# A graph network block on one core: node loops written out, chunks of four tiles, units of eight, a ring of six

## The reference

```python
seg = edge_type * N_NODES + dst
def _rgcn_layer(x, W, root, bias, src, dst, seg):
    agg = jax.ops.segment_sum(x[src], seg, num_segments=N_REL * N_NODES)
    agg = agg.reshape(N_REL, N_NODES, -1)
    return jnp.einsum('rnd,rde->ne', agg, W) + x @ root + bias
```

## Time and profile before

| | us |
|---|---|
| Median of 3 runs | 10040.12 (10038.99 to 10089.25) |
| Profiled execution, its span | 10274.9 |
| PE busy | 6298.0 (61%) |
| POOL busy | 4692.1 (46%) |
| DVE busy | 2244.8 (22%) |
| ACT busy | 1095.0 (11%) |

### The profile page before, as it was taken

How to read it: one execution, slowest core, us unless ns; L and a number is a source line. 1 busy time by engine, 2 the same in 40 slices (tenths; PEclk the granted TensorE clock), 3 DMA queues, 4 the chain that set the end, 5 groups by cost and what they waited for, 6 DMA issues and landing times.

```text
span 10274.9 us, 106460 instructions
## 1 busy us (share of the span) xinstructions
PE 6298.0 (61%) x23187; PEld 4307.1 (42%) x23188; DVE 2244.8 (22%) x6475; ACT 1095.0 (11%) x2855; POOL 4692.1 (46%) x4958
## 2 busy tenths in 40 slices
PE   5866556555556666666666665664666665556666
PEld 2333333333333334444444444443444444444445
DVE  2311111111111122222222221222222222222222
ACT  1110000000000000000000000010111111111111
POOL 0134555554555544444444444445444444444443
PEclk9977777777777777777777777777777777777777
DMA  4443333333333333333332323323222222222222
GB/s 120 131 123 95 93 93 98 99 94 93 95 93 96 97 89 89 92 91 91 90 91 87 90 87 93 89 86 97 67 73 67 69 68 71 72 70 69 67 68 60
DMA packets 410721, 899.60 MB, mean 88 GB/s; under 512 B 149828, under 2 KB 236588, under 8 KB 391946
## 3 DMA queue, kind: packets, MB, share of 16 engines
q0 software_dynamic: 232128, 634.17, 21.4%
q10 hardware_dynamic: 116050, 257.82, 8.2%
q1 hardware_dynamic: 62518, 7.30, 0.6%
HBM read 704.42 MB, written 192.01 MB: 87 GB/s over the span
## 4 chain that ended last, share of the span: by engine, by line
PE 38%; issue 29%; another core or an unknown queue 27%; DVE 2%; ACT 2%; ACTq 1%; DVEq 1%; DMA 1%; POOL 0%; POOLq 0%; SPq 0%; PEld 0%; PEldq 0%
PE ps_out L1169 17%; PE ps_y L1130 8%; PE ps_y L1344 3%; PE ps_tr L1286 2%; PE ps_b L1355 2%; PE ps_c L1355 2%; DVE onehot L849 1%; PE ps_tr L1108 0%; PE ps_out L1183 0%; ACT L713 0%; DVEq L849 0%; PE ps_b L1274 0%; PE ps_c L1230 0%; DVEq L885 0%
## 5 line engine op out<-in xcount | busy, mean ns | idle before, releaser
L447 POOL DMA_INDIRECT ring<-table,idx_now x4836 | 4634.1, 958 | 4979.6 <-PEq L1180 3530.7
L1169 PE MATMUL ps_out<-ring,onehot 128*125 x10848 | 3342.2, 461 | 2881.1 <-issue 1772.5
L1169 PEld LDWEIGHTS ps_out<-ring,onehot 128*125 128x125 f32 x10848 | 2290.8, 225 | 3938.9 <-issue 3574.5
L849 DVE TENSOR_TENSOR onehot<-targets,nodes_now 128x250 f32<-128x250 f32 x2712 | 1131.5, 422 | 5341.1 <-remote 2955.1
L1130 PE MATMUL ps_y<-W,hT 128*125 128x512 f32 (+1 forms) x3000 | 1347.1, 600 | 17.5 <-DVE y_stage L739 16.4
L1130 PEld LDWEIGHTS ps_y<-W,hT 128*125 128x125 f32 x3000 | 598.9, 207 | 606.7 <-issue 560.5
L1344 PEld LDWEIGHTS ps_y<-hT,big 128*128 128x128 f32 x3200 | 440.2, 207 | 25.4 <-issue 4.7
L1355 PE MATMUL ps_b<-big,gT 128*125 128x256 f32 x800 | 268.1, 467 | 294.6 <-ACT gT L713 282.2
L1344 PE MATMUL ps_y<-hT,big 128*128 128x125 f32 x3200 | 444.5, 291 | 5.5 <-issue 5.4
L462 ACT COPY y_stage<-ps_y 125x512 f32<-125x512 f32 x450 | 263.5, 585 | 1002.0 <-PE ps_y L1130 973.3
L1286 PE MATMUL ps_tr<-W,gT 128*125 128x256 f32 x800 | 258.2, 493 | 94.6 <-ACT gT L663 94.6
(11 more groups left out here) (172 smaller groups left out, 2819.1 us busy)
## 6 DMA issues: line engine op xcount, KB each, us to landing
table<-y_stage ACTq DMA_DIRECT2D x150, 1008.0 KB
ring<-table,idx_now POOLq DMA_INDIRECT x4836
base_in<-table ACTq DMA_DIRECT2D x150, 125.0 KB
table<-y_stage ACTq DMA_DIRECT2D x150, 117.0 KB
x_in<-in_x_dram ACTq DMA_DIRECT2D x100, 125.0 KB
xn_in<-xn_scratch ACTq DMA_DIRECT2D x100, 125.0 KB
xn_scratch<-xn_in ACTq DMA_DIRECT2D x50, 125.0 KB
res_scratch<-res_win ACTq DMA_DIRECT2D x50, 125.0 KB
```

Source lines behind the costliest of these rows:

```text
L447: nc.gpsimd.indirect_dma_start(ring[:, c * D:(c + 1) * D], None, table[l], bass.IndirectOffsetOnAxis(ap=idx_now[:, c:c + 1], axis=0)).then ...
L849: nc.vector.tensor_tensor(onehot[u][:, :, :], targets[:, bass.ds(col + u * TILES, TILES)].unsqueeze(2).broadcast_to([128, TILES, WIN]), no ...
L1169: mm = nc.tensor.matmul(ps_out[0:WIN, 0:D], onehot[u][:, j, :], ring[:, bass.ds(slot + j * D, D)], start=(start and u == 0 and j == 0), st ...
```

## The change

The five numbers are set anew: four tiles in a chunk (a chunk is 512 edges), two chunks in a unit (eight tiles, 1,024 edges; `UNIT` itself stays), a ring of six chunks (24 tiles, where it was 26), and three chunks in SP's first group of indices. `windows` becomes a Python loop, so that each engine's program holds the 50 windows one after the other; the inner loop over units, whose bounds come from the data, stays a loop.

```diff
-TILES = 2
-RING = 13
+TILES = 4
+RING = 6
 UNIT = 2
-GROUP_A = 7
+GROUP_A = 3
...
-            body((0, 0, 0), None)
-            with eng.Fori(0, NW // 2 - 1) as i:
-                body((i * 2 + 1, 1, i), (i * 2, 0, i))
-                body((i * 2 + 2, 0, i + 1), (i * 2 + 1, 1, i))
-            last = (NW - 1, 1, NW // 2 - 1)
-            body(last, (NW - 2, 0, NW // 2 - 1))
+            last = None
+            for w in range(NW):
+                cur = (w, w % 2, w // 2)
+                body(cur, last)
+                last = cur
             tail(last)
```

## The result

The changed kernel takes **10,888.65 us** (median of 4 runs, 10,888.12 to 10,900.18) against 10,052.5 us (4 runs) for the kernel before: 1.083 times as long, with an interval of 1.081 to 1.085, or 836 us more. I had forecast 355 us more.

A forecast was written before the change was run, and what follows sets the result against it. The prediction put the time in waits between engines, repeated in 147 window steps. Steps +340, padding +75 and register rows -60 gave +355 us, added to the median of 10,040 for 10,395 us; range 9,450 to 11,000.

The forecast's parts named there:

- its matrices wait for late releases: Fifth unit of a layer 1 window: its one-hot matrices wait for PE's signals, 12.5 and 13.6 us late.
- G: Moment in a window's step when the first slots come back and gathers start, 5.8 us after the first matmul.
- 24 gathers, to G + 29.7: POOL in a window: gathers for the fourth to sixth units run without a pause, ending 29.7 us after G.
- the result's signal comes 8.7 us later: From sum's end to ACT: 8.7 us where gathers have started again, the middle of 2.5 and 14.9.
- first rival: Window step: faster by fewer late releases, fifth unit's first chunk waiting only for data; step 55 us, 9,450 us; chance 0.24.
- second rival: Window step: much slower, lateness per matmul or POOL never pausing while signals wait; step 65.5 us, 11,000 us; chance 0.14.
- +2.3 us carried to all layers: Window steps: layer 1's growth from 59.1 to 61.4 us applied to all 147 steps, +340 us.
- The median: Whole kernel: the profiled execution is 2.3% above the median of 10,040 us; the 355 us were added to the median.
- Padding, +75 us: End of each layer: edge list padded to 1,632 gathers instead of 1,612, so the last window ends later, +75 us.
- Register rows, -60 us: Written-out windows: about five register rows a window leave PE's path at 0.08 us each, -60 us.
- Look-ahead: Window start: 16 instead of 22 tiles lie ahead; without late releases this alone would cost 7.5 us more on that path.
- What would show it: New profile's signs: 61.4 us steps in layer 1, runs of 24 gathers, one 10 us pause, 1,632 gathers a layer.

The follow-up runs named there:

- r3: Kernel before with units of eight tiles and a ring of 24, chunks still of two tiles, on chip A: 10,236.3 us, ratio 1.019.
- e8: Changed kernel, but a window's last unit of slots given back only after its transposes (layer 3: next window's start), chip A: 9,724.5 us, ratio 0.967.
- r2: Changed kernel with a window's last slots given back only after the transposes, run again on chip A: 9,728.8 us, ratio 0.969.
- t2: Kernel before, loops kept, with the changed numbers and the last unit's slots given back only after the transposes, chip B: 10,027.3 us, ratio 0.980.
- s2: Kernel before with windows written out, old numbers, and the last unit's slots given back only after the transposes, chip B: 10,081.3 us, ratio 0.989.
- s3: Kernel before, loops kept, with the last unit's slots given back only after the transposes, chip B: 10,150.4 us, ratio 0.995.
- e1: Kernel before with only the loops over windows written out, numbers as before, chip A: 10,009.5 us, ratio 0.996.
- e3: Kernel before with only the ring one chunk shorter (12 chunks of two tiles), loops kept, chip A: 10,123.3 us, ratio 1.008.
- e4: Kernel before with units of eight tiles and a ring of 24, chunks still of two tiles, chip C: 7,807.5 us, ratio 1.136.
- r4: Kernel before with chunks of one tile, units of four and a ring of 26 tiles, chip A: 10,644.3 us, ratio 1.061.
- e11: Changed kernel with the last unit's slots given back after the transposes, in layer 3 already after the activation's signal, chip C: 8,069.0 us, ratio 1.174.
- e7: Kernel before with chunks of one tile, units of four and a ring of 26 tiles, chip C: 6,819.8 us, ratio 0.992.
- e9: Kernel before with the last unit's slots given back only after the window's transposes, chip C: 6,876.1 us, ratio 1.000.

## Why the prediction was wrong

The direction held, and the time lies in the whole range, but outside the forecast's own 10,150 to 10,750: 836 us more, where I had 355. The step that failed is "its matrices wait for late releases: 8.6 + 12.5 = G + 21.1, and 13.6 + 13.6 = G + 27.2". The signals of the fourth unit's two chunks, which I took to be 12.5 and 13.6 us late as in the earlier trace rows, came within 0.2 us. With it fell what hung on it: the run of "24 gathers, to G + 29.7", and the term "the result's signal comes 8.7 us later", which was 18.7. By the steps, for the window shown (G = 2336.66):

| | forecast | measured |
|---|---|---|
| first matmul to G | 5.8 | 6.0 |
| fourth unit's chunks | G + 6.7, G + 11.7 | G + 7.4, G + 12.4 |
| fifth unit's chunks | late, 21.1 and 27.2 or later | G + 17.4, G + 22.4 |
| end of the sum | G + 31 or 37 | G + 26.2 |
| end of the run of gathers | G + 29.7 | G + 40.8 |
| ACT has the result | G + 39.6 | G + 45.7 |
| rest, to the next first matmul | 15.4, and 0.6 for L1183 | 15.0 (L1182 is ahead of ACT's row) |
| step | 61.4 | 66.7 |

The sum ended 5 to 11 us sooner than forecast, because no one-hot matrix on the path was late; that is what the first rival counted on for its first chunk. But the two units given back in time (POOL's rows at 2349.69 and 2359.72 are released by line 1179) carried the run on to 32 gathers. The signal, sent at G + 26.2 + 0.8, had to wait for the run's end and 5.0 us more: 18.7 us where I had 8.7. The two mistakes have opposite signs, and the second is larger. The second rival of the prediction, "POOL never pauses and signals wait for it", names what happened, at a price of 65.5 us a step where layer 1 has 65.1; I gave it 0.14. That its 11,000 is near the time is in part luck: it adds 6.4 us to all 147 steps of the profiled kernel, where the layers have 6.0, 4.6 and 2.9. The argument that I set against it, that a longer wait also stops POOL sooner, holds for late matrices (r3) and not for a late result: while the run lasts, nothing that POOL needs hangs on the result. e8, r2 and t2 take the long run away, and the loss goes with it.

- **8.7 us as the middle of 2.5 and 14.9.** Two windows of 150 were read the earlier trace rows, and I took the second for one without gathers. It isn't: its matmul ends at 2372.6, some 6 us into a run that goes from 2366.45 to 2381.2. So whether gathers run doesn't alone say how late a signal is. 2.5 is the mean of layer 1, and 14.9 the worst of all 150; the middle of the two was far too high for the kernel before (1.5 us on average) and too low for the changed one (16.6). s2 and s3 failed on the same number.
- **+2.3 us carried to all layers.** Between the two profiles it was +6.0, +4.6 and +2.9. These sum to 49 x 13.5 = 660 us, of which the last steps have 144; the spans differ by 612, since the stretches ahead of the layers and between them got some 50 us shorter.
- **The median.** The profiled execution before is 2.3% above its median, that of the changed kernel is at it (10,888.3 against 10,888.65). Adding 355 to the median took for granted that the changed kernel has the same surplus, and it doesn't: 836 - 612 = 224 us of the miss of 481; the other 257 are the steps. On which chip that profile was taken isn't on record. e1, which is within 0.4% of the kernel before, shows the plainer comparison: on chip A its layer 1 has steps of (3509.5 - 698.2)/49 = 57.4 us, against 65.1.
- **Padding, +75 us:** 4,896 gathers and 1,518 matrices are there as counted. e3, which has the same 60 gathers more and hardly another change in its steps, costs 81 us (0.6 to 1.0%), so the size was about right; in the changed kernel itself the three last steps took 144 us more.
- **Register rows, -60 us:** e1 measures -43 us (-29 to -56, by its ratio of 0.9957, 0.9944 to 0.9971) for all that writing out does. No row stood behind the "up to some 100 us" for bringing the code in; no such cost shows. By the rule of the Trainium skill (Runtime: NRT & Kernel Launch, "Instruction fetch mechanics"), a stall at a taken branch out of the two-page window, my estimate was -190. The measured gain is less than a quarter of that, and doesn't say what it is made of.
- **Look-ahead:** without late signals units of eight cost 13.6% (e4 on chip C), with them 1.9% (r3), padding counted in both. That the waits hide the rest is likely, but not shown.
- **What would show it:** gathers, matrices, the 5 us between the fourth unit's chunks, and DVE's remote waits above 1,500 us (2,299.7) were right; the steps of layers 2 and 3 (69.9 and 68.6 for 68) were near. Steps of 61.4 us in layer 1 (65.1), runs of 24, one pause of 10 us (24.3 here) and the fifth unit's chunks 6 to 12 us apart (5.0) were wrong.

**Open.** Why the signals are late. The traces show only "remote" and that on chips A and B lateness comes with runs of gathers. Why chip C has none of it at the same 1.25 us a gather is open too; the granted clock is 0.91 there and 0.77 on chip A, and no run tells whether that is a cause or follows from PE's shorter waits. What the traces do show is where in a run the signals begin to be late. Medians over the runs of 16 gathers or more, of the start of the matrix that takes the freed buffer less the end of the chunk's last matmul, and of that end's place in the run:

| PE's chunk signal in the run | before (chunks of 2) | changed (chunks of 4) | r4 (chunks of 1) |
|---|---|---|---|
| 5th | 0.1 us late, 4.3 us into the run | 0.2 late, at 14.5 | 0.1 late, at 2.9 |
| 6th | 0.8 late, at 5.3 | 7.6 late, at 21.1 | 0.2 late, at 3.3 |
| 7th | 4.8 late, at 6.2 | 20.5 late, at 24.5 | 0.1 late, at 3.8 |
| 10th | 8.7 late, at 20.1 | too few | 3.3 late, at 5.5 |

Time into the run alone doesn't decide: a signal at 14.5 us comes at once in the changed kernel, and one at 6.2 us is 4.8 us late in the kernel before. That is what I had wrong when I carried the 12.5 us over. The number of signals fits better for chunks of two and four, which both have five in time, but r4 has eight. So neither is the rule by itself.

**The best version** on chip A is the changed kernel with the pause: 9,724.5 us, 0.967 of the kernel before (again 0.969 in r2). It wasn't run on chip B; there its looped form t2, 0.980, was best. On chip C its near relative e11 was 1.174; there chunks of one tile (e7, 0.992) were best, which cost 6.1% on chip A (r4).

## What to carry to other kernels

Ask of a faster step what it sets free next: here releases that came in time let a side engine run on across the stage's end, and the stage's own result was queued behind it. A limit that looks like a loss (slots held back, 8 tiles for some 11 us) can be worth 11% where signals are late, and brought nothing to the kernel before, late signals (0.995) or not (1.000); so state on which chip a number was read, and run the kernel before in turn with each experiment. When a wait has two faces in the trace, count over all windows which is usual before taking the middle of two rows. And look at the last window by itself: a ring of another size pads the work to another length.

## What the runs showed of the hardware

- The same kernel takes 10,042, 10,201 or 6,877 us on three chips, each stable within 1% over 6 to 13 runs. The gathers cost 1.25 us from start to start on all three; the difference that the traces show is in the arrival of PE's signals while gathers run: no result was late in any of the 600 windows of e4, e7, e9 and e11 on chip C.
- A result's signal came 18.7 us after the matmul and 5.0 us after a run of 32 gathers, 9.6 and 4.0 us with a run of 24 (e8), and within 0.1 us when sent 2.7 us into a run (r3), in one window each; the means of a layer are 16.2 to 16.8 us in the changed kernel and 0.9 to 2.5 in the kernel before.
- e1, written out with the same numbers, fetches 231 packets of instruction code instead of 25 and is 0.4% faster; what the packets cost by themselves isn't shown.
